# New slot tables for an attention kernel, and two PSUM banks in turn for the first projections

## The reference, cut to what matters

```python
xn = _layernorm(x)
q = (layernorm(xn) * norm_g + norm_b) @ Wq        # 16 heads of 64
k, v = split(xn @ Wkv, 2)
k, v = concat([null_k, k]), concat([null_v, v])   # two null positions
q, k = l2norm(q) * q_scale, l2norm(k) * k_scale
sim = q @ k.T * 8 - slope[h] * distance           # causal
out = softmax(sim) @ v @ Wout
x = x + out + (second layer, here a normalised copy of xn with ln_g, ln_b)
```

## Time and profile before

| what | value |
| --- | --- |
| median of 3 runs | 2789.91 us (2785.57 to 2790.7) |
| profiled execution, its own time | 2793.3 us |
| span of the profiled execution | 2791.3 us |
| mean granted TensorE clock | 0.987 |
| TensorE busy | 2646.4 us, 95% of the span |
| VectorE busy | 2555.2 us, 92% |
| ScalarE and GpSimd busy | 2132.3 us (76%) and 2174.8 us (78%) |

### The profile page before, as it was taken

How to read it: one execution, slowest core, us unless ns; L and a number is a source line. 1 busy time by engine, 2 the same in 40 slices (tenths; PEclk the granted TensorE clock), 3 DMA queues, 4 the chain that set the end, 5 groups by cost and what they waited for, 6 DMA issues and landing times. The chain is left out here.

```text
span 2791.3 us, 84780 instructions
## 1 busy us (share of the span) xinstructions
PE 2646.4 (95%) x31631; PEld 1570.5 (56%) x31631; DVE 2555.2 (92%) x6760; ACT 2132.3 (76%) x3385; POOL 2174.8 (78%) x2438
## 2 busy tenths in 40 slices
PE   5689999999999999999999999999999999999997
PEld 3355555555555555555655555555555555555554
DVE  7799999999999999999989999999999999899996
ACT  5477787777777788777877778877777777777775
POOL 6696878877788687977879778897778868798663
PEclk7899999999999999999999999999999999999999
DMA  5222354423533244434443235433354333542222
GB/s 185 42 49 52 72 102 87 82 64 71 95 104 69 61 75 92 108 60 67 89 89 95 52 75 101 86 88 59 69 102 97 69 69 69 89 103 55 50 50 65
DMA packets 629574, 220.17 MB, mean 79 GB/s; under 512 B 593584, under 2 KB 595632, under 8 KB 629168
## 3 DMA queue, kind: packets, MB, share of 16 engines
q1 hardware_dynamic: 627696, 214.67, 37.4%
q10 hardware_dynamic: 1472, 0.09, 0.0%
HBM read 55.23 MB, written 16.78 MB: 26 GB/s over the span
## 5 line engine op out<-in xcount | busy, mean ns | idle before, releaser
L1027 DVE CUSTOM_DVE_ANT_0 PS<-PS,STR 128x512 f32<-128x512 f32 (+3 forms) x1536 | 822.3, 580 | 82.1 <-PE PS L1275 72.9
L589 ACT ACTIVATE AR<-PS,SC 128x1024 f32<-128x1024 f32 (+1 forms) x640 | 653.6, 1021 | 164.8 <-PE PS L1286 100.4
L1228 PE MATMUL PS<-WH,XT 128*128 128x388 f16 x2048 | 680.2, 332 | 38.2 <-DVE AR L1040 31.4
L1230 PE MATMUL PS<-WH,XT 128*128 128x388 f16 x2048 | 677.9, 331 | 0.0
L1229 PE MATMUL PS<-WL,XT 128*128 128x388 f16 x2048 | 677.4, 331 | 0.0
L593 ACT ACTIVATE AR<-AR 128x1024 f16<-128x1024 f32 (+1 forms) x640 | 621.8, 972 | 20.3
L799 POOL TENSOR_TENSOR RN<-SS,HALF 128x8 f32<-128x8 f32 x256 | 450.4, 1760 | 165.8 <-DVE SS L1112 163.9
L1068 DVE TENSOR_TENSOR AR<-AR 128x768 f16<-128x768 f32 (+1 forms) x448 | 546.6, 1231 | 9.4 <-ACT AR L593 9.0
L1251 PE MATMUL PS<-AR 64*128 64x512 f16 (+3 forms) x4608 | 496.2, 324 | 19.9 <-ACT AR L589 19.4
L1313 PE MATMUL PS<-AR 128*128 128x66 f16 x4608 | 474.4, 196 | 3.2 <-DVE AR L1068 1.9
L1315 PE MATMUL PS<-AR 128*128 128x64 f16 x4608 | 470.3, 192 | 0.0
(11 more groups left out here) (221 smaller groups left out, 5210.8 us busy)
## 6 DMA issues: line engine op xcount, KB each, us to landing
XW<-in_L_attn_x SPq DMA_DIRECT2D x112, 256.0 KB, 3.0
out<-ACC SPq DMA_DIRECT2D x64, 256.0 KB, 2.2
ACC<-in_L_attn_x SPq DMA_DIRECT2D x56, 256.0 KB, 2.9
AR<-QKB SPq DMA_TRANSPOSE x512, 2.5
AR<-in_L_attn_Wkv SPq DMA_DIRECT2D x2, 1536.0 KB, 12.5
ACC<-in_L_attn_x SPq DMA_DIRECT2D x2, 1024.0 KB, 7.3
AR<-in_L_attn_Wout SPq DMA_DIRECT2D x1, 2048.0 KB, 9.3
AR<-CTK SPq DMA_TRANSPOSE x128, 2.4
```

Of the source, the lines that this page charges most:

```text
L589: e.activation(PR[:, n % 2, :, 0:wide], SB[:, :, 0:wide], ACT.Exp, scale=SIG).then_inc(s_p, 1)
L1027: e.tensor_tensor_reduce(out=r[:, 0:n], in0=r[:, 0:n], in1=ST[:, u % 2, h, o:o + n], scale=1.0, scalar=LOW, op0=ALU.add, op1=ALU.max, accu ...
L1228: e.matmul(PJ, XT[:, k, xs], WH[:, k, p, :], start=k == 0, stop=False)
L1230: ins = e.matmul(PJ, XT[:, 4 + k, xs], WH[:, k, p, :], start=False, stop=k == KC - 1)
```

## The change

All tables get new numbers. In addition the projection tiles alternate between two PSUM banks while the running tile number is below 12 (the eight tiles of the first unit and four of the second): odd tiles go to bank 3, which belongs to `AV` and is not used before the first unit's values. TensorE then waits for the evacuation of the tile before the last one. The first write into `AV` waits for the first 12 tiles instead of for an earlier division.

```diff
+TWO_PJ = 12
-W_OTT = [106, 150]
+W_OTT = [120, 152]
-HOLD = [8.7, 9.8, 8.8]
+HOLD = [6.9, 7.8, 7.7]
-W_LATA = [-188, -181, -162, -132, -132, -87, -83, -83, -72, -66, 14, 23, 33, 55, 61, 64]
+W_LATA = [-300, -294, -270, -254, -238, -215, -167, -149, -109, -106, -103, -48, -34, -32, 53, 68]
...
-        SB, AV, PJ = PS[:, 0:2, :], PS[:, 2:4, 0:264], PS[:, 4, 0:WC]
+        SB, AV = PS[:, 0:2, :], PS[:, 2:4, 0:264]
...
+        def pj(i):
+
+            return PS[:, 3 if i < TWO_PJ and i % 2 else 4, 0:WC]
...
-                    if i:
-                        w.wait_ge(s_kvev, 2 * i)
-                        w.wait_ge(s_qb, i)
-                        w.wait_ge(s_vl, i)
-                e.matmul(PJ, XT[:, k, xs], WH[:, k, p, :], start=k == 0, stop=False)
+                    old = i - 1 if i < TWO_PJ else i
+                    if old > 0:
+                        w.wait_ge(s_kvev, 2 * old)
+                        w.wait_ge(s_qb, old)
+                        w.wait_ge(s_vl, old)
+                e.matmul(pj(i), XT[:, k, xs], WH[:, k, p, :], start=k == 0, stop=False)
...
-                    w.wait_ge(s_on, 2 * u + qc)
+                    if u or qc:
+                        w.wait_ge(s_on, 2 * u + qc)
+                    else:
+                        w.wait_ge(s_kvev, 2 * TWO_PJ)
+                        w.wait_ge(s_qb, TWO_PJ)
+                        w.wait_ge(s_vl, TWO_PJ)
```

More of the change, by code:

```diff
@@ new lines @@
+W_PLOW = [96, 101, 102, 106, 113, 114, 125, 130, 133, 140]
+W_VALUE = [105, 107, 109, 116, 125, 131, 134, 145, 145, 148]
+W_NVP = [102, 114]
+W_ON = [106, 145]
+W_OTS = [109, 149]
+W_OTL = [107, 148]
+W_OTT = [120, 152]
+W_OP = [121, 124, 141, 148, 159, 159, 170, 172]
+W_ADD = [120, 122, 137, 145, 155, 157, 167, 167]
+W_PROJ = [z for z in [5, 10, 16, 22, 28, 35, 41, 49] for k in range(KC)]
+W_KV = [5, 10, 16, 24, 34, 35, 42, 46]
+W_VL = [4, 7, 16, 20, 28, 31, 40, 46]
+W_STRIP = [34, 44]
+W_SQ = [12, 26, 44, 51]
@@ new lines @@
+W_SS = [11, 20, 40, 50]
+W_POW = [20, 32, 47, 52]
+W_TP = [34, 40, 56, 72]
+W_HI = [28, 39, 54, 70]
+W_LO = [28, 33, 53, 65]
+W_ROWS = [67, 93]
+W_SHIFT = [68, 90]
+W_CTP = [79, 99]
+W_NX = [78, 97]
+W_NL = [73, 99]
+W_NTT = [87, 106]
+W_XA = [-358, -309, -250, -202, -180, -146, -115, -88]
+W_STAT = [-290, -207, -181, -171, -126, -97, -93, -88]
+W_XB = [-89, -76, -48, -12, -1, 2, 13, 18]
+W_XF = [-67, -29, -28, -12, -3, -2, 16, 22]
+W_XH = [-58, -20, -16, -6, 1, 11, 30, 33]
+W_XL = [-53, -22, -22, -8, 5, 5, 23, 29]
@@ new lines @@
+W_XTP = [-37, -12, 2, 4, 14, 22, 33, 37]
+W_SMALL = [-82, -77, -76, -71, -71]
+W_VSC = [-61]
+W_BASE = [80, 80, 96, 103, 112, 123, 131, 156]
+W_BN = [82, 89, 100, 109, 122, 131, 142, 183]
+W_BM = [82, 89, 97, 110, 117, 132, 151, 179]
+W_BA = [85, 92, 100, 112, 123, 141, 162, 187]
+HOLD = [6.9, 7.8, 7.7]
+W_LATA = [-300, -294, -270, -254, -238, -215, -167, -149, -109, -106, -103, -48, -34, -32, 53, 68]
+W_LATD = [-257, -230, -173, -161, -131, -119, -94, -88, -85, -33, -13, 25, 36, 54, 68, 92]
+W_XF0 = [-276, -174]
@@ L111 @@
+W_XH0 = [-70, 5]
+W_XL0 = [-168, -94]
+W_XT0 = [-133, -20]
+W_WOS = [-169]
+W_VNA = [-233, 13]
+W_VND = [11]
+W_ALP = [-99, 33]
+W_ALA = [20]
+W_WOM = [29, 36, 46]
+W_WOT = [48, 52]
+W_WOA = [63, 69, 78, 91]
+W_WOD = [60, 65, 69, 87]
 SLOTS = range(-500, SL * NU + 200)
@@ L1038, in _ @@
                         w.wait_ge(s_nsc, g - 2)
-                    e.tensor_tensor(QKB[:, g % 3, t % 2, 128:260], PJ[:, 128:260], BQF[:, u % NP, :], ALU.add).then_inc(s_qb, 1)
+                    e.tensor_tensor(QKB[:, g % 3, t % 2, 128:260], pj(i)[:, 128:260], BQF[:, u % NP, :], ALU.add).then_inc(s_qb, 1)
                     e.scalar_tensor_tensor(
-                        out=V[:, i % NV20, :, 72:136], in0=PJ[:, 260:388].rearrange("p (j c) -> p j c", j=2),
+                        out=V[:, i % NV20, :, 72:136], in0=pj(i)[:, 260:388].rearrange("p (j c) -> p j c", j=2),
                         scalar=VSC[:, b % 2, 1, t:t + 1], in1=V[:, i % NV20, :, 0:64], op0=ALU.mult,
```

36 lines of the change are left out of this document (7 added, 29 removed).

## The result

The changed kernel takes 2744.37 us (median of 4 runs, 2743.14 to 2749.21) against 2787.74 us of the kernel before in the same measurement. The ratio is 0.9845, with a 95% interval of 0.983 to 0.9861, so 43 us are won. The forecast was 2768 us with a range down to 2745: the sign was right, the gain was twice the forecast, and the time lies 0.6 us outside the range.

A forecast was written before the change was run, and what follows sets the result against it. In the steady part neither TensorE nor VectorE was taken as the bound alone; time is lost handing over banks. 2793.3 - 10 (start) - 12 (steady part) = 2771 us as profiled, 2768 us for the median; range 2745 to 2788 us.

The forecast's parts named there:

- The start: First unit: with two banks P1 follows P0 at once and P8 comes 11 to 12 us sooner; 10 us taken.
- 3.7 us won: First unit: P2 starts at 65 us against 68.73 before; the lower bound of the gain there.
- some 1 us: First unit: three more splits beside GpSimd's work, contending for memory, would make the gain there some 1 us less.
- The waits for VectorE's evacuation: Sign of being right: TensorE's waits for line 1045 stay below 12 us in total.
- VL6 too late for P7: Sign of being wrong: TensorE waits for line 1045 in units after the second.
- Slower: Rival, steady part: VL6 behind MAX11 comes 1.0 us later; at 0.7 us per unit 2823 us; chance 0.13.
- MAX11's mechanism: Steady part: PLOW9 lies beside GpSimd's power, not its 512-wide multiplication, takes about 1 us; M1's 0.78 us wait goes.
- The filled wait: Steady part: MAX11 ahead of VL6 uses the 0.35 us in which VectorE waited for ScalarE.
- The other reorderings: ADD3, M2, the output tiles and BA3: put at nothing, each moving within a stretch whose reader comes later.
- the halving of the 24 us to 12: Steady part: half of 24 us taken, since a TensorE gaining at M1 finds other banks not yet free.
- the bound of 36.2 us: Steady part: upper bound of the gain, all TensorE waits for a maximum ahead of the 256-column pieces M1 and M7.
- The rival rules: Skill rules: PSUM double buffering gives nothing at the start; GpSimd contention takes some 1 us there, steady part as taken.

The follow-up runs named there:

- MAX11 alone: Kernel before with one number changed, so that MAX11 stands ahead of VL6 and the sum of squares: 2775.29 us, ratio 0.9957.

## Why the prediction was wrong, point by point

**The start: the sum was right, in part by luck.** The term of 10 us measured 9.7 us with the bank alone; with the new tables it is 13.4 us, inside the bounds of 3.7 to 18 us. P8 was to start at 86 us and came at 85.73. But P2 was to come 16.6 us after P0 and came 19.9 us after it, so the "3.7 us won" at P2, the lower bound, measured 0.4 us. The splits are why: they were counted at 2.2 us more, and the last three alone took 3.7 us more than their count, beside GpSimd. The forecast named this neighbour and gave it "some 1 us". The six tiles behind made up for it: they took 19.3 us instead of 21.2, with 3.0 us of waiting at the 4.41 us maximum instead of 4.4, and P0 itself came 1.8 us sooner.

**Two signs were wrong.** The waits for VectorE's evacuation were to stay below 12 us in total. That was a slip where it concerns P1, whose wait does not go but moves to P2 (13.07 us of the 32.0). But a wait for line 1045 in units after the second was named as a sign of being wrong, "VL6 too late for P7", and it is there: 10.8 us, nearly all of it in the third unit of the sequences, 0.64 us ahead of P4 and 0.85 us ahead of P7. The rival *Slower* happens in one unit of eight.

**MAX11's mechanism was right.** PLOW9 fell from 1.81 to 0.95 us in the unit shown and MAX0 came in time. The mean of the group fell from 1121 to 1029 ns. Counted over the trace of before, 120 of the 768-wide subtractions lay mostly beside GpSimd's power and took 0.94 to 0.96 us; 46 lay mostly beside its 512-wide multiplication and took 1.51 us in the mean, up to 1.81. The filled wait, 0.35 us in the forecast, is worth 13 of the 40 us; how the other 27 divide between the neighbour and the bank that comes free sooner is not shown.

**The failed step** is this one: "The other reorderings (ADD3, M2, the output tiles, BA3) I put at nothing: the number of instructions and of changes between tile shapes on TensorE is the same, and each moves within a stretch in which its reader comes later." With it went the halving of the 24 us to 12. Priced one at a time on the kernel before, the terms of the sum were good: forecast 10, 12 and 0 (BA3), measured 9.7, 11.3 and 0 us, 21 us in sum. ADD3, also put at nothing, cost 28 us there. But the tables change together, and there O2's place is worth 11 us, BA3 16 us, and O3 with ADD3 52 us, each as measured by taking it back. Taken back singly the pieces come to 13 + 40 + 11 + 52 + 16 = 132 us for a change worth 43. So these are not shares: an order taken back in part fits worse than either whole order. The tables alone won 28.8 us, and the steady part became 31.9 us shorter by the windows, where 12 were forecast; the bound of 36.2 us held.

**The halving held on the old order and not on the new.** The forecast held that a TensorE that gains at M1 finds other banks not yet free. With MAX11 alone that is what happened: TensorE's waits for a maximum fell from 48.7 to 29.5 us and those for VectorE's evacuation rose from 31.4 to 39.8. With all tables such waits came too, the 10.8 us above, but the idle time as a whole fell: from the fourth unit to the last TensorE is busy 2429.8 of 2464.5 us, where it was 2433.5 of 2496.4, so 34.7 us are left of 62.9. VectorE's wait for pieces rose from 64.2 to 75.3 us between 300 and 2700 us, and its wait for ScalarE fell from 51.6 to 41.2. A wait of VectorE's for TensorE's work was no sign of a wait on TensorE to come.

**The rival rules.** The Trainium skill's "TensorE: Matmul & The Clock Gate", section HAM oscillation, reports a kernel in which PSUM double buffering gave no further gain; here the bank alone brought 9.7 us, so this kernel's start does not agree. By the Trainium skill's "GPSIMD Engine Reference", section Specifications, GpSimd contends with VectorE's operations of two SBUF inputs; the runs agree (VectorE's subtraction 1.22 to 2.29 us), and show it for GpSimd's operations too (1.28 to 2.13 us).

**What stays open.** Which of the reorderings closes the way from the kernel before with MAX11 alone (11 us) to the tables alone (29 us) was not built up from below, only taken back from above. Several were never taken back, and the list ahead of the prediction leaves some of them out. By the tables, value step 4 now stands behind P4 on TensorE and the float16 half of group 0 ahead of PLOW6 on VectorE in 62 units, ADD6 stands behind the sum of squares of group 1 in 30, and M2 moved in 63. In units 16 to 55, 260 of the 1120 pieces and output tiles follow another one in their bank. What these are worth no run shows. Why BA3 counts only on the new tables is open as well.
